# The head of a decoder layer: which transfers go first, on which queue, and which operand is split first

## The reference, cut to what matters

```python
qk = x @ W_qk                      # [4096, 128] @ [128, 1024]
q, k = jnp.split(qk, 2, axis=-1)
v = x @ W_v
dots = jnp.einsum('bhid,bhjd->bhij', q, k) * SCALE
dist = jnp.clip(seq[None, :] - seq[:, None], -MAX_POS, MAX_POS) + MAX_POS
bias = conv[:, dist]               # conv is [8, 21]
attn = jax.nn.softmax(dots + bias[None], axis=-1)
```

## Time and profile before

| | |
|---|---|
| Time, median of 3 runs | 449.33 us (447.81 to 451.22) |
| Time of the profiled execution | 447.76 us |
| Its span, first to last instruction | 445.7 us |
| PE busy | 421.6 us, 95% of the span |
| DVE, ACT, POOL busy | 317.2, 298.1, 190.2 us |
| First matmul that works on x's product (`z_mm(0, 0)`) | 9.03 us after the span's start |

### The profile page before, as it was taken

The page is one execution under the profiler, slowest core; times in us unless marked ns, Lnnn a source line. Parts: engine busy times, 40 slices in busy tenths (PEclk is TensorE's granted clock), DMA queues, the critical chain, the costliest instruction groups (busy, mean ns, idle before and its releaser), DMA issues.

```text
span 445.7 us, 14337 instructions
## 1 busy us (share of the span) xinstructions
PE 421.6 (95%) x5098; PEld 365.9 (82%) x5099; DVE 317.2 (71%) x999; ACT 298.1 (67%) x649; POOL 190.2 (43%) x220
## 2 busy tenths in 40 slices
PE   7999999989998899999988999989998999999994
PEld 6688888878887776776665898989998999999963
DVE  5568888888888878989897668885444445443964
ACT  4678778768767498987965976336665665336654
POOL 5620220220810012221858665645777766554430
PEclk9999999999999999999999999999999999999999
DMA  4343242850000005311212225221232432326436
GB/s 139 88 132 83 57 109 57 178 163 1 4 2 26 2 26 177 101 40 46 69 62 67 62 73 131 74 55 41 76 91 79 107 90 80 84 74 200 168 120 189
DMA packets 47630, 38.11 MB, mean 86 GB/s; under 512 B 5088, under 2 KB 40928, under 8 KB 47568
## 3 DMA queue, kind: packets, MB, share of 16 engines
q1 hardware_dynamic: 42816, 28.16, 23.5%
q0 software_dynamic: 4320, 8.92, 5.9%
q10 hardware_dynamic: 432, 0.20, 0.2%
HBM read 19.30 MB, written 16.34 MB: 80 GB/s over the span
## 4 chain that ended last, share of the span: by engine, by line
PE 52%; DVE 26%; ACT 9%; issue 7%; DMA 3%; POOL 2%; DVEq 1%; SPq 0%; ACTq 0%; POOLq 0%
PE bank L1503 7%; PE bank L1471 5%; PE bank L1461 5%; PE bank L1416 4%; DVE tkr L1636 2%; DVE negmax L1645 2%; DVE prob L1642 2%; PE bank L1077 2%; PE bank L1130 2%; PE bank L1120 2%; PE bank L1079 2%; DMA routed<-rh,zbuf 2%; PE bank L1078 2%; PE bank L1490 2%; PE bank L1492 2%
## 5 line engine op out<-in xcount | busy, mean ns | idle before, releaser
L661 POOL DMA_INDIRECT routed<-rh,zbuf x71 | 70.5, 993 | 45.6 <-DVE rh L2060 29.8
L2060 DVE TENSOR_SCALAR rh<-bank,zbuf 128x128 f32<-128x128 f32 x71 | 24.8, 349 | 44.1 <-PE bank L1503 21.9
L1503 PE MATMUL bank<-wdn,prob 128*128 x384 | 47.3, 275 | 1.3 <-DVE rh L2060 1.3
L1503 PEld LDWEIGHTS bank<-wdn,prob 128*128 128x128 f32 x384 | 45.2, 192 | 1.7 <-DVE rh L2060 1.7
L557 POOL DMA_INDIRECT slots<-zbuf,slot x32 | 33.3, 1041 | 18.1 <-issue 5.8
L994 ACT ACTIVATE prob<-bank 128x512 f32<-128x512 f32 x48 | 28.6, 597 | 16.2 <-PE bank L1492 13.5
L557 POOL DMA_INDIRECT slots<-tkr,slot x32 | 32.1, 1004 | 13.1 <-issue 5.5
L694 ACT ACTIVATE prob<-prob 128x512 f32<-128x512 f32 x32 | 20.2, 630 | 15.9 <-DVE prob L1646 15.8
L1490 PE MATMUL bank<-xT_hi,wq_hi 128*128 128x256 f32 x96 | 29.0, 302 | 1.3 <-DVE xT_lo L2070 1.3
L1416 PEld LDWEIGHTS bank<-sdn,qblk 128*128 128x128 f32 x256 | 29.7, 192 | 0.5
L1416 PE MATMUL bank<-sdn,qblk 128*128 128x128 f32 x256 | 29.9, 275 | 0.0
(11 more groups left out here) (338 smaller groups left out, 1206.1 us busy)
## 6 DMA issues: line engine op xcount, KB each, us to landing
slots<-x2T SPq DMA_DIRECT2D x8, 585.0 KB, 5.2
zbuf<-slots SPq DMA_DIRECT2D x24, 130.0 KB, 2.5
tkr<-in_x SPq DMA_DIRECT2D x8, 256.0 KB, 3.1
cs<-in_ctx SPq DMA_DIRECT2D x8, 256.0 KB, 2.9
wup<-in_L_ffn_routed_up SPq DMA_DIRECT2D x1, 2048.0 KB, 8.6
zbuf<-tkr SPq DMA_DIRECT2D x8, 256.0 KB, 2.7
out_x<-x2T SPq DMA_DIRECT2D x8, 256.0 KB
tkr<-routed SPq DMA_DIRECT2D x6, 256.0 KB, 3.3
```

What stands on the lines that cost most here:

```text
L661: pool.indirect_dma_start(routed, bass.IndirectOffsetOnAxis(ap=xr[n][:, :].bitcast(I32)[:, DEST:DEST + 1], axis=0), yr[n % 4][:, :], None) ...
L1503: m = mm(bank[6 + a][:, 0:D], hTp[:, q, c // 2, c % 2, a, :], wdn[:, bass.ds(e * (FC * D) + c * D, D)], start=(c == 0), stop=(c == FC - 1))
```

## The change

Transfers: SP issues `w_qk` first and no longer issues `cin` and x's group 0; ACT issues these two, ahead of `wv`, `wo` and `bout`. SP waits for `cpad_ok` and stores `cpad` right after `gw`, ahead of `load_x(1)` and the four small loads. Splits: ACT and DVE do the query parts of the weights, then x's group 0, then the key parts. PE: four warm matmuls instead of six after `x_turn(0)`, and the gate transposes stand after the second product.

```diff
@@ block.sync
-        sp.dma_start(cin[:, :], conv).then_inc(s["ld_conv"], 16)
-        load_x(0)
         sp.dma_start(wqk, w_qk).then_inc(s["ld_wqk"], 16)
-        load_x(1)
         sp.dma_start(gw[0:NH, :], w_ig).then_inc(s["ld_gw"], 16)
         sp.dma_start(gw[NH:2 * NH, :], w_fg).then_inc(s["ld_gw"], 16)
+        sp.wait_ge(s["cpad_ok"], 3)
+        sp.dma_start(conv_pad, cpad[:, :]).then_inc(s["stored"], 16)
+        load_x(1)
...
-        sp.wait_ge(s["cpad_ok"], 3)
-        sp.dma_start(conv_pad, cpad[:, :]).then_inc(s["stored"], 16)
         sp.wait_ge(s["stored"], 16)
@@ block.scalar
         act.preload_act_table_set("natural_log_exp_and_others")
+        act.dma_start(tok[:, 0:GT, :], x_tok[:, 0:GT, :]).then_inc(s["ld_tok"], 16)
+        act.dma_start(cin[:, :], conv).then_inc(s["ld_conv"], 16)
         act.dma_start(wv[:, :], w_v).then_inc(s["ld_attn"], 16)
...
-        act.wait_ge(s["xT_ps"], 1)
-        act.activation(xT_hi[0][:, :], bank[7][:, :], ACT.Copy).then_inc(s["xhi_ok"], 1)
-        act.wait_ge(s["ld_wqk"], 16)
-        for w in range(2):
+        def wq_high(w):
             for e in range(2):
                 act.activation(wq_cut[0][:, w, :, e, :], wqk_cut[:, w, :, e, :], ACT.Copy,
                                scale=DQ ** -0.5 if w == 0 else 1.0).then_inc(s["wq_ok"], 1)
+        act.wait_ge(s["ld_wqk"], 16)
+        wq_high(0)
+        act.wait_ge(s["xT_ps"], 1)
+        act.activation(xT_hi[0][:, :], bank[7][:, :], ACT.Copy).then_inc(s["xhi_ok"], 1)
+        wq_high(1)
@@ block.tensor
-        warm(6)
-        pe.wait_ge(s["ld_gw"], 32)
-        for c in range(3):
-            m = pe.transpose(bank[6][:, 8 * c:8 * c + 8], gw[:, c * D:(c + 1) * D], ident[0:8, 0:8])
-        m.then_inc(s["prep_ps"], 1)
+        warm(4)
         for h in range(H):
...
             z_mm(0, h)
+            if h == 1:
+                pe.wait_ge(s["ld_gw"], 32)
+                for c in range(3):
+                    m = pe.transpose(bank[6][:, 8 * c:8 * c + 8], gw[:, c * D:(c + 1) * D], ident[0:8, 0:8])
+                m.then_inc(s["prep_ps"], 1)
@@ block.vector
-        dve.wait_ge(s["xhi_ok"], 1)
-        tt(xT_lo[0][:, :], bank[7][:, :], xT_hi[0][:, :], ALU.subtract).then_inc(s["xlo_ok"], 1)
-        for w in range(2):
+        def wq_low(w):
...
+        wq_low(0)
+        dve.wait_ge(s["xhi_ok"], 1)
+        tt(xT_lo[0][:, :], bank[7][:, :], xT_hi[0][:, :], ALU.subtract).then_inc(s["xlo_ok"], 1)
+        wq_low(1)
```

## The result

The changed kernel took **449.84 us** (median of 20 runs, 447.81 to 451.82), the kernel before 446.92 us in as many runs beside it (444.95 to 451.22). The ratio is **1.0058, 95% interval 1.0040 to 1.0075**: slower by 2.6 us, between 1.8 and 3.4 (the two medians by themselves lie 2.9 us apart). That is within 1%, at the place where the forecast put it, and more than the 1.1 us that the forecast gave the difference. The profiled execution took 451.82 us.

A forecast was written before the change was run, and what follows sets the result against it. PE, busy 421.6 of 445.7 us, was taken as the bound, so head delays reach the end: +0.97 (splits behind late `cin`) and +0.1 (gate transposes) make +1.1 us on the 449.33 median, 450.4; range 447.9 to 452.0.

The forecast's parts named there:

- Step 3: `cin` behind x lands with it at 5.2; DVE's 2.41 us prologue is no longer hidden and ends at 7.66.
- Step 1: x's first group, issued 0.45 us earlier, takes turns with `w_qk` packet by packet and lands at 5.2.
- Rival A: x and `cin` land by 4.7, so DVE's query parts start before POOL's add: 448.5 to 449.0 us; chance 0.32.
- Step 4: DVE's first `wq_lo` part meets POOL's add, `xT_lo` ends near 9.96, first product at 10.0 instead of 9.03: +0.97 us.
- Step 5: Gate transposes between products 1 and 2 on PE, partly in a gap: cost 0 to 0.35, taken as 0.1 us.
- Steps 2, 6 and 7: Head: earlier `w_qk`, two warm matmuls less, and SP's `cpad_ok` wait ahead of the second x: no cost.
- rival C: TensorE at 1.2 GHz when products start: up to 5.5 us, 1 us if it rises soon after 10; chance 0.06.

The follow-up runs named there:

- e1: The changed kernel with `cin` issued first of all on SP instead of behind x on ACT: 445.49 us, ratio 0.9972 to the kernel before.
- f3: The changed kernel with `cin` first on SP and eight warm matmuls instead of four behind `x_turn(0)`: ratio 0.9973 to the kernel before.
- f4: The changed kernel run and profiled a second time, no edit: ratio 1.0084 to the kernel before.
- e2: The changed kernel with ten instead of four warm matmuls behind `x_turn(0)`: 449.61 us, ratio 1.0068 to the kernel before.
- f1: The changed kernel with queues swapped, x's first group and `cin` first on SP, `w_qk` first on ACT: ratio 1.0081 to the kernel before.
- e4: The kernel before, transfers as they were, with only the changed order of splits, gate transposes and four warm matmuls: ratio 1.0033.
- f2: The kernel before with `cin` issued behind x's first group on the same queue instead of ahead of it: ratio 1.0043.
- g2: The kernel before, profiled a third time, no edit: first product at 7.88 us, first scores at 16.43.

## Why the prediction was right, and where its size was off

Sign, place and size of the whole came as forecast: 449.84 us against 450.4. The difference between the kernels did not: +1.1 us was forecast, 2.6 (1.8 to 3.4) measured. The forecast time came out close because the three runs that it was added to had a median of 449.33, and 20 runs have 446.92.

**Step 3, the late `cin`: right.** It landed 0.2 us behind x, DVE's prologue took 2.38 us (5.89 to 8.27; 2.41 forecast), and it was not hidden. e1 gives back 2.8 us of the head by moving this transfer, with x's earlier landing in it; no run moved `cin` and nothing else, and its own share, some 1.8 us, is an estimate.

**Step 1, x beside `w_qk`: the turns right, the start wrong, and half a microsecond off.** x landed at 5.69 (5.2 forecast, from two sums of 4.9 and 6.0). The sum had both queues moving packets from the same moment. In the changed kernel x moved none until 3.25, then took turns with `w_qk`, then had the engines to itself. That the forecast came so near has some luck in it: 5.2 was a choice between the two sums, and the late first packet is in neither as such. Rival A, a landing of 4.7 or less, was not seen in any of the six profiles of kernels that issue the two together. e1 issues `w_qk` 0.46 us behind x and lands x at 3.53. The rule of the Trainium skill that was set against the row ("DMA: Bandwidth & Descriptors", section Issuing engines are not separate DMA queues: another engine only saves time on the sequencer) would have had x land at 4.26. The traces do not bear it out here: with 0.46 us of head start x took 2.7 us (e1) and 3.0 (f3), without it 4.9.

**Step 4, the splits: the sum right, two terms wrong against each other.** The prologue ended at 8.27, not 7.66, and so the first part of `wq_lo` met only the end of POOL's add: 702 ns, a hold of 0.3 us where about 1.0 was forecast. `xT_lo` ended at 9.95 (9.96 forecast), the product started at 10.08 (10.0).

**Step 5: 0.2 instead of 0.1 us.** With fast passes the transposes take 0.28 in f4's profile and e1's, and the pass behind them 0.43 where before the gap made it 0.49.

**Steps 2, 6 and 7: right by what was seen.** The weights were ready at 4.55, no wait on x's second group or on `hankel` appeared, and the wait for `lnw` was covered. Whether the two warm matmuls less cost anything is not settled: e2 and f3 add some and gain nothing in the median, and e2's executions had a lower granted clock than the changed kernel's.

**Where the size failed, first: rival C.** It had a chance of 0.06. It came in two profiles of three, and cost 1.66 us in the first and 1.3 in the third (first scores at 20.17 against 18.84), near the lower of the two prices that the prediction had for it ("If it comes soon after 10, 1 us"). It should have stood in the sum with a weight, not among the unlikely. The prediction put it down to PE's idle time from about 8 to 10. The profiles don't show that cause: PE was idle before the first product for 1.53 and 1.60 us in the two with passes of 0.43, and for 1.82 (f1), 2.33 (e4) and 2.76 us (f4) in three with passes of 0.23. In f4 and e4 the weight loads were fast before the gap (192 ns) and the passes behind it were too. In the first two and f1 they took 333 ns before it, and behind it both levels occur. In the nine others, with less idle time in one piece, the products start fast (in f2 the level fell later). The Trainium skill ("TensorE: Matmul & The Clock Gate", Part 1) says that the number of slow matmuls at a kernel's start differs between runs of one kernel; f4 against the other two profiles agrees.

**Second: the kernel before.** The sum took 9.03 us, from one profile, as its start. g2 shows that the same kernel also starts at 7.88, when DVE's second part is ahead of POOL's add. The margin stood in the rows: POOL's add at 7.52 and the long part at 7.56. The prediction read the hold and its 1.0 us from there, but not that an execution can miss it.

Over three profiles each, the first scores start at 17.59, 17.62 and 16.43 before (mean 17.2) and at 20.47, 18.84 and 20.17 after (mean 19.8): **2.6 us**, which is what was measured. With three profiles each that agreement may be partly luck. Behind the head the first profiles keep their distance of 2.9 us up to 88 us. The kernel before then loses 1.5 us near 94, at the place that e4 shows above, and the changed one loses 1.4 and 1.2 in the stretches of lower clock at 140 and 230 to 240 us. Such stretches come at up to four places in an execution, and the places differ between profiles of one kernel, before and after the change; the median of an execution's mean clock is 0.992 and 0.990 in two groups of the kernel before, 0.994 in both of the changed one. So they can't be put down to the change.

**Open:** why x's first packet comes so late in the changed kernel and not in f1; what settles TensorE's level at the first product; how often the meeting of DVE and POOL near 94 us is lost, and whether that and the clock explain the medians of e2 and e4; why f2's last weight packets were late; what brings the stretches of lower clock in the middle.

## What to carry to other kernels

Before a tiny transfer is moved behind a big one, check what stands behind its wait: 672 bytes held 2.4 us of constants that nothing else needed to wait for, and put first they cost nothing. Where a wait is won or lost by a few hundredths of a microsecond, one profile gives one of two kernels; take several before using its start as the base of a sum. The level at which TensorE starts its products can differ between executions of one kernel, and it was worth 1.3 to 1.7 us here; where it is in doubt, it belongs in the sum with its chance.

## What the runs showed of the hardware that was not expected

- 0.46 us of head start went with a transfer of x (256 KB) of 2.7 us (e1) and 3.0 (f3), against 4.9 with `w_qk` 0.02 us ahead (changed kernel).
- Two loads issued 0.02 us apart on two queues can start moving some 1.5 us apart: x had its first packet between 3.2 and 3.5 us in all five profiles of the changed transfers, `w_qk` at 1.9. Once both moved, they took turns (23 packets against 22 in a quarter of a microsecond; 24 against 24 in f1).
- 672 bytes behind 256 KB on the same queue landed with them: 4.5 us (changed kernel) and 2.8 us (f2) after the issue, against 1.4 alone.
- The granted clock of a window reads 1.00 from 10 to 13 us in the changed kernel while its passes take 0.43 instead of 0.23 us, before any fast weight load was seen; in f2, where fast passes came first, it reads 0.50 for passes of the same 0.43.
- The meeting of DVE and POOL costs either side, but not alike: the part of `wq_lo` that started 0.04 us behind the add took 1422 ns instead of 410; the add that started behind such a part took 1.34 us instead of 1.18 (g2).
- Within a kernel whose TensorE is busy for 95%, the clock falls at up to four places in an execution for some microseconds (0.66, 0.73 and 0.59 in three windows of 5 us).
